# Expert tiles packed across two images: 39 tiles in place of 46, nine of them before the second image is routed

## The chip, the cores and the metric

The kernel runs on one core of a Trainium2 chip. The metric is the device time of one execution in microseconds (us), as the median of several executions. The core has five engines that run side by side and wait for each other through semaphores: TensorE (PE in the profile, PEld its weight loads), VectorE (DVE), ScalarE (ACT), GpSimd (POOL) and SyncE (SP). SP, ACT and POOL also issue DMAs.

## The reference, cut to what matters

Two images of 128 channels and 32 x 32 pixels pass through an attention block over pixels (4 heads), a linear attention block (8 heads) and a mixture of experts with top-2 routing. The last part is the one that the change touches:

```python
t = t + _L1_ffn_ref(_ln_t(t), Wr, br, ln_g, ln_b, W1, b1, W2, b2)    # t: 2 images x 1024 tokens x 128

def _L1_ffn_ref(x, Wr, br, ln_g, ln_b, W1, b1, W2, b2):             # E = 8 experts, hidden size 512
    probs = softmax(xt @ Wr + br)
    top_p, top_idx = top_k(probs, 2)
    weights = top_p / top_p.sum(axis=-1, keepdims=True)
    xn = (xt - mu) * rsqrt(var + LN_EPS)
    xe = xn[None] * ln_g[:, None, :] + ln_b[:, None, :]
    h = gelu(einsum('end,edh->enh', xe, W1) + b1[:, None, :])
    y = einsum('enh,ehd->end', h, W2) + b2[:, None, :]
    out = (weights[:, :, None] * y[chosen two experts]).sum(axis=1)
```

Every token goes to two of eight experts, so each image brings 2048 rows. How many rows an expert gets is known only at run time.

## The kernel before, in words

All is written by hand: each engine has one program, and the order in it is the order of the code. The image is called b (0 the first, 1 the second).

**Attention.** 64 steps (`UNITS * STEPS`) of scores on PE, exponentials on ACT (L558) and products with the values on PE (L864). Beside them a second stream finds the row maxima ahead of time (PE L806, L826; DVE L1189). These maxima go through `mrow` and two DMAs on SP (`max_rows`, L352) into `Qs`, and the scores of each half unit (L845) wait for them. From step 33 on (`LAYER1_AT`), the first image's later layers are spread between the steps: projection, linear attention, router, and at step 56 the counting.

**Routing, per image.** `v_slots(b)` on DVE turns the counts into a seat for each row in a table `expert_in` in DRAM (`xs`): rows of an expert stand together, each expert's share is padded to whole tiles of 128 rows, and each image has its own region of `TILES` = 23 tiles. POOL then writes the rows there with 16 indirect DMAs per image (`scatter`, L491: 8 token groups by 2 choices). The padding rows were written before, in `expert_in <- zeros` (L478); they hold zeros and the number of an unused result row. `v_slots` also makes `tab` (the expert of each tile), `etab` and `affine` (layer-norm scale and shift of each tile).

**The order on POOL.** Zero fill (L472 to L478), a wait for it, then `rsqrt` twice for the first image, `scatter(0)` with the first `rsqrt` of the second image (`rsqrt(B + 2)`) put before the last two of its 16 DMAs, `rsqrt(B + 3)`, four `send`s, `scatter(1)`, and the other 42 sends. Image 1's token layer norm (DVE L1239, `F`) waits for `rsqrt(B + 2)`.

**Expert tiles.** A loop over `NT` = 46 tiles runs on every engine (`expert_step`). For tile s: SP loads it into one of 8 buffers (`load_tile`, L378); PE transposes it (L1042); ACT copies it with the expert's scale and shift (L666); PE makes the hidden layer (L1068, four matmuls in two passes each); DVE adds the bias (`H`, L1469); ACT applies gelu (L684); PE makes the result of tile s - 1 (L1081); DVE adds its bias (`Y`, L1480); POOL sends it to DRAM rows (`send`, L496). The tiles of image 1 wait for all of `scatter(1)` (L389: `scattered[1]`), those of image 0 for `scatter(0)`. The second image's later layers (`LAYER1_PE`, `LAYER1_DVE`, `LAYER1_ACT`) are laid before and between the first six tile steps; its `v_slots` comes on DVE after tile step 4.

**The end.** SP waits for the sends, loads the results back (`load_sent`, L385), PE sums residual and gated results (L1098 to L1108), ACT copies, SP stores.

```python
TILES = (2 * L + E * (P - 1)) // P        # 23: the most tiles that one image can need
NT = B * TILES                            # 46
```

## Time and profile before

| | us |
|---|---|
| median of 3 runs (363.18 to 363.31) | 363.25 |
| span of the profiled execution | 384.2 |
| PE busy in it | 334.2 |
| DVE busy | 202.1 |
| ACT busy | 204.4 |
| POOL busy | 110.8 |

The profile is of one execution, and its span is 21 us longer than the median of the timed ones. The mean granted clock of TensorE over the span is 0.929 of the full 2.4 GHz; where it is below 1 it is at the lower of its two levels, 1.2 GHz, for part of the time. In the rows, a number in brackets behind a line is the time for which the engine sat idle before it, and an arrow names what ended that idle time; "remote" and "another core or an unknown queue" mean that the profile found no releaser, and "issue" that it shows nothing the engine waited for.

### The profile page before, as it was taken

Reading aid. Unit: us, or ns where it says so; the run is one execution under the profiler, and the core shown is the slowest. Engines: PE = TensorE matmul, PEld = TensorE weight load, DVE = VectorE, ACT = ScalarE, POOL = GpSimd, SP = SyncE. Lnnn points to the kernel's source line nnn. Section 1 sums busy time; section 2 is a strip of 40 time slices with the busy share of each in tenths; the row PEclk is TensorE's granted clock in tenths of the full one; section 3 lists DMA queues with packets and bytes.
Section 4 is the critical chain, followed back from the end, with each engine's and each line's share of the span. In section 5 each row is a group of like instructions: output and inputs, shape, how many; then the busy total and the mean of one; then the engine's idle time right before and its main releaser. Section 6 shows DMA issues by size and latency. Waiting matters only on the chain.

```text
span 384.2 us, 6582 instructions
## 1 busy us (share of the span) xinstructions
PE 334.2 (87%) x2004; PEld 211.5 (55%) x2004; DVE 202.1 (53%) x616; ACT 204.4 (53%) x324; POOL 110.8 (29%) x140
## 2 busy tenths in 40 slices
PE   7879799899999989999998496967551999999996
PEld 3533343333333335445432354867551999999996
DVE  2584444563756553565576248666402455777620
ACT  1460765666576554655585023665212677777732
POOL 2082291000000001000307630061774344444430
PEclk9985989999999999999999879996665899999999
DMA  6078768660000025000001102010211222222415
GB/s 186 2 149 194 170 146 333 154 243 34 0 2 3 3 72 149 0 2 1 2 0 43 55 8 62 16 28 23 62 62 34 64 72 70 71 66 79 143 37 210
DMA packets 21772, 29.28 MB, mean 76 GB/s; under 512 B 4055, under 2 KB 15628, under 8 KB 21484
## 3 DMA queue, kind: packets, MB, share of 16 engines
q1 hardware_dynamic: 16808, 18.04, 17.7%
q0 software_dynamic: 3744, 10.31, 8.4%
q10 hardware_dynamic: 1188, 0.53, 0.6%
q8 instruction: 17, 0.28, 0.3%
q14 instruction: 15, 0.12, 0.1%
HBM read 11.62 MB, written 9.25 MB: 54 GB/s over the span
## 4 chain that ended last, share of the span: by engine, by line
PE 70%; DVE 13%; issue 6%; another core or an unknown queue 4%; ACT 3%; DMA 1%; POOL 1%; DVEq 0%; SPq 0%; ACTq 0%; POOLq 0%
PE ps L864 15%; PE ps L1081 10%; PE ps L1068 9%; PE ps L845 6%; PE ps L826 6%; DVE above L1189 4%; PE ps L706 2%; PE ps L806 2%; PE ps L922 2%; PE ps L746 2%; PE ps L899 2%; PE ps L778 1%; PE ps L891 1%; DMA Qs<-mrow 1%
## 5 line engine op out<-in xcount | busy, mean ns | idle before, releaser
L558 ACT ACTIVATE probs<-ps 128x1024 f32<-128x1024 f32 x64 | 65.3, 1021 | 37.0 <-PE ps L845 36.9
L1081 PE MATMUL ps<-w,GT 128*128 x368 | 55.0, 297 | 18.8 <-ACT GT L684 15.0
L864 PE MATMUL ps<-probs,vT 128*32 128x512 f32 x256 | 68.2, 608 | 1.1 <-ACT probs L558 1.1
L864 PE MATMUL ps<-probs,ones 128*32 128x512 f32 x256 | 68.2, 609 | 0.0
L1081 PEld LDWEIGHTS ps<-w,GT 128*128 128x128 f32 x368 | 49.3, 208 | 22.0 <-issue 21.7
L1189 DVE CUSTOM_DVE_ANT_0 above<-ps,above 128x512 f32<-128x512 f32 x56 | 38.7, 691 | 40.8 <-PE ps L826 39.0
L496 POOL DMA_INDIRECT token_out<-Y,yidx x46 | 44.2, 961 | 48.2 <-DVE Y L1480 46.6
L433 POOL TENSOR_TENSOR rstd<-ve,minus_half 128x1 f32<-128x1 f32 (+2 forms) x6 | 10.3, 1724 | 160.6 <-DVE ve L1231 88.6
L1068 PE MATMUL ps<-XTT,w1s 128*128 128x128 f32 x368 | 53.1, 291 | 3.2 <-issue 3.2
L684 ACT ACTIVATE GT<-H 128x512 f32<-128x512 f32 x46 | 28.9, 629 | 46.5 <-DVE H L1469 27.4
L1068 PEld LDWEIGHTS ps<-XTT,w1s 128*128 128x128 f32 x368 | 49.2, 208 | 4.3 <-issue 4.3
L551 ACT ACTIVATE above<-ps 128x512 f32<-128x512 f32 x56 | 33.5, 599 | 25.3 <-PE ps L806 25.3
L1469 DVE TENSOR_TENSOR H<-ps,b1T 128x512 f32<-128x512 f32 x46 | 31.8, 691 | 27.8 <-PE ps L1068 7.4
L845 PE MATMUL ps<-Qs,Ks 98*128 98x512 f32 x128 | 44.0, 425 | 1.8 <-DMA Qs<-mrow 1.1
L845 PEld LDWEIGHTS ps<-Qs,Ks 98*128 98x128 f32 x128 | 21.8, 191 | 31.0 <-issue 23.7
L491 POOL DMA_INDIRECT expert_in<-X,slots x32 | 31.0, 969 | 25.4 <-DVE slots L1374 16.3
L826 PEld LDWEIGHTS ps<-Ks,Qs 96*128 96x128 f32 x56 | 10.6, 190 | 38.1 <-DVE pm L1189 32.8
L826 PE MATMUL ps<-Ks,Qs 96*128 96x512 f32 x56 | 28.0, 500 | 3.5 <-DVE pm L1189 1.4
L659 ACT ACTIVATE w1s<-w 128x512 f32 x46 | 28.5, 619 | 0.5 <-issue 0.4
L1480 DVE TENSOR_TENSOR Y<-ps,bias 128x128 f32<-128x128 f32 x46 | 13.3, 290 | 23.3 <-remote 11.1
L666 ACT ACTIVATE XTT<-ps,affine 128x128 f32<-128x128 f32 x46 | 20.3, 442 | 9.5 <-PE ps L1042 9.5
L806 PE MATMUL ps<-Kd,Qs 96*128 96x512 f32 x56 | 23.4, 418 | 1.0 <-ACT above L551 1.0
(196 smaller groups left out, 427.5 us busy)
## 6 DMA issues: line engine op xcount, KB each, us to landing
expert_in<-zeros POOLq DMA_DIRECT2D x2, 1495.0 KB, 7.6
XR<-expert_in SPq DMA_DIRECT2D x46, 65.0 KB
Qs<-q_hi SPq DMA_DIRECT2D x16, 128.0 KB, 3.1
w<-in_L_ffn_W SPq DMA_DIRECT2D x1, 2048.0 KB, 8.4
w<-in_L_ffn_W SPq DMA_DIRECT2D x8, 256.0 KB, 4.1
YG<-token_out SPq DMA_DIRECT2D x8, 256.0 KB, 4.1
Ks<-k_hi SPq DMA_DIRECT2D x14, 128.0 KB, 2.6
X<-in_x SPq DMA_DIRECT2D x2, 512.0 KB, 4.6
```

Source lines behind the costliest of these rows:

```text
L491: pool.indirect_dma_start(xs[:, :], bass.IndirectOffsetOnAxis(ap=slots[:, b, w, j:j + 1], axis=0), X2[:, b, j, :], None).then_inc(scattere ...
L496: pool.indirect_dma_start(yt[:, :], bass.IndirectOffsetOnAxis(ap=yidx[:, t:t + 1], axis=0), Y[:, t % NBY, :], None).then_inc(y_sent[t % NB ...
L551: nc.scalar.activation(above[:, n % 2, :], bank(slot_banks(g)[1]), ACT.Relu).then_inc(above_ready, 1)
L558: nc.scalar.activation(probs[:, s % 3, :], bank(2 + 2 * (s % 2), 2), ACT.Exp).then_inc(exp_done, 1)
L806: nc.tensor.matmul(bank(slot_banks(g)[1]), q, Kd[0:SPLIT, b, n, :], start=True, stop=True).then_inc(diff_ready, 1)
L826: last = nc.tensor.matmul(o, Qs[0:SPLIT, b, n, t * P:(t + 1) * P], Ks[0:SPLIT, b, n, HALF:L], start=True, stop=True)
L845: last = nc.tensor.matmul(bank(2 + 2 * (s % 2) + hd), Ks[0:STACK, b, n, kt * P:(kt + 1) * P], Qs[0:STACK, b, n, qh * HALF:(qh + 1) * HALF] ...
L864: last = nc.tensor.matmul(bank(6 + o % 2)[i * HD:(i + 1) * HD, :], w, probs[:, s % 3, hd * HALF:(hd + 1) * HALF], start=kt == 0, stop=kt = ...
L1068: last = nc.tensor.matmul(bank(2 + s % 2)[:, c * P:(c + 1) * P], w1s[:, s % 2, c, :], XTT[:, s % NB, :], start=True, stop=True)
L1081: last = nc.tensor.matmul(bank(4 + p)[:, 0:D], GT[:, p, c, :], w2[:, e, c, :], start=c == 0, stop=c == HC - 1)
L1189: nc.vector.tensor_tensor_reduce(above[:, n % 2, :], bank(base), above[:, n % 2, :], scale=1.0, scalar=-3.0e38, op0=ALU.add, op1=ALU.max, ...
L1469: nc.vector.tensor_tensor(H1[:, s % NB, :].rearrange("p (c t) -> p c t", c=HC), bank(2 + s % 2).rearrange("p (c t) -> p c t", c=HC), b1T[: ...
```

## The change

The two images no longer have a region each. `FULL` = 9 tiles is the least number of whole tiles that 2048 rows over 8 experts must contain; `REST` = 30 is the most that is then needed for all that is left of both images; `NT` = 39.

- `v_slots(0)` gives the first image's whole tiles the tiles 0 to 8 (whole tiles beyond the ninth, and each expert's incomplete rest, go to the tiles from 9 on, padded), in `seats_own`. It then notes where free seats are (`seats_left`).
- `v_slots(1)` puts the second image's rows into the free seats first and into new tiles behind them (`seats_filled`).
- Tiles 0 to 8 wait for `scatter(0)`, tiles 9 to 38 for `scatter(1)`.
- At the border the loop takes tiles in another order: after tile 8's hidden layer the results of tiles 7 and 8 are both made, and then the tiles 9 and 10 are fetched (`tiles_closed`, `tiles_fetched`).
- The zero fill has 39 tiles in place of 46, in two DMAs of 20 and 19 tiles from a smaller buffer, the second issued after the first has landed.
- The results of tiles 0 to 22 (`OWN`) are waited for before the first image's results are loaded back, as before.

The diff, cut to its core:

```diff
-    TILES = (2 * L + E * (P - 1)) // P
-    NT = B * TILES
+    OWN = (2 * L + E * (P - 1)) // P
+    FULL = -(-(2 * L - E * (P - 1)) // P)
+    REST = (B * 2 * L - FULL * P + E * (P - 1)) // P
+    NT = FULL + REST
+    TILE_RANGE = ((0, FULL), (FULL, NT))
+    ZT = 20
+    ZEROED = ((0, ZT), (ZT, NT))
...
+        def tiles_fetched(s):
+            if FULL - 2 <= s < FULL:
+                return (FULL, FULL + 1) if s == FULL - 1 else ()
+            return (s + 2,) if is_tile(s + 2) else ()
+
+        def tiles_closed(s):
+            if s == FULL - 1:
+                return (s - 1, s)
+            return () if s == FULL or not is_tile(s - 1) else (s - 1,)
...
             for t in range(NT):
-                if t % TILES == 0:
-                    sp.wait_ge(scattered[t // TILES], 16 * 2 * J)
+                if t in (0, FULL):
+                    sp.wait_ge(scattered[t // FULL], 16 * 2 * J)
                 load_tile(t)
...
-            for b in range(B):
-                v = xs[b * TILES * P:(b + 1) * TILES * P, :].rearrange("(p r) d -> p r d", p=P)
-                pool.dma_start(v, zeros[:, :, :]).then_inc(xs_zeroed, 16)
-            pool.wait_ge(xs_zeroed, 16 * B)
+            for i, (first, end) in enumerate(ZEROED):
+                rows = end - first
+                link(nc.gpsimd.iota(zeros[:, 0:rows, D], ...))
+                v = xs[first * P:end * P, :].rearrange("(p r) d -> p r d", p=P)
+                pool.dma_start(v, zeros[:, 0:rows, :]).then_inc(xs_zeroed, 16)
+                pool.wait_ge(xs_zeroed, 16 * (i + 1))
...
+            def seats_own(n):
+                link(nc.vector.tensor_copy(cnt_i[:, :], n))
+                whole_tiles(WHOLE)
+                running(CUM, WHOLE)
+                link(nc.vector.tensor_tensor(BEFORE, CUM, WHOLE, ALU.subtract))
+                nc.vector.tensor_scalar_min(CUTS, CUM, float(FULL * P))
+                link(nc.vector.tensor_scalar_min(AT, BEFORE, float(FULL * P)))
+                link(nc.vector.tensor_tensor(CUT, CUTS, AT, ALU.subtract))
+                link(nc.vector.tensor_tensor(LEFT, n, CUT, ALU.subtract))
+                link(nc.vector.tensor_scalar_add(cnt_i[:, :], LEFT, float(P - 1)))
+                whole_tiles(PAD)
+                running(CUMPAD, PAD)
+                link(... START ...)
+                link(nc.vector.tensor_tensor(SHIFT, START, CUT, ALU.subtract))
+                link(nc.vector.tensor_tensor(SHIFT, SHIFT, AT, ALU.subtract))
...
             def v_slots(b):
...
-                link(nc.vector.tensor_scalar_add(cnt_i[:, :], incl[:, :, J - 1], float(P - 1)))
-                link(nc.vector.tensor_scalar(cnt_i[:, :], cnt_i[:, :], 7, 7, ALU.arith_shift_right, ALU.logical_shift_left))
-                link(nc.vector.tensor_copy(cnt[:, 0, :], cnt_i[:, :]))
-                link(nc.vector.tensor_tensor_scan(cnt[:, 1, :], ones[:, 0:E], cnt[:, 0, :], 0.0, ALU.mult, ALU.add))
-                link(nc.vector.tensor_tensor(cnt[:, 2, :], cnt[:, 1, :], cnt[:, 0, :], ALU.subtract))
-                link(nc.vector.tensor_tensor(slotv, slotv, cnt[:, 2, :]..., ALU.add))
+                if b == 0:
+                    seats_own(incl[:, :, J - 1])
+                else:
+                    seats_filled(incl[:, :, J - 1])
                 link(nc.vector.tensor_tensor(slotv, slotv, ps[...], ALU.add))
+                link(nc.vector.tensor_tensor(past, slotv, over_j(CUT), ALU.is_ge))
+                nc.vector.tensor_tensor(slotv, slotv, over_j(AT), ALU.add)
+                link(nc.vector.tensor_tensor(past, past, over_j(SHIFT), ALU.mult))
+                link(nc.vector.tensor_tensor(slotv, slotv, past, ALU.add))
```

**DVE, first image's seats.** What stands between the running sum over the counts (L1361 before, L1433 after) and the first multiplication with the chosen experts (L1372, L1445). `xn` is scratch for the 64-wide seats, `cnt` for the 8-wide counts. Before:

```order
L1362 TENSOR_SCALAR cnt_i<-xn 128x8
L1363 TENSOR_SCALAR cnt_i<-cnt_i 128x8
L1364 CAST cnt<-cnt_i 128x8
L1365 SCALAR_TENSOR_TENSOR cnt<-ones,cnt 128x8
L1366 TENSOR_TENSOR cnt<-cnt 128x8
L1367 TENSOR_TENSOR xn<-xn,cnt 128x64
L1369 TENSOR_TENSOR xn<-xn,ps 128x64
```

Now, the last twelve of 21 rows (nine more 8-wide ones stand ahead of them):

```order
L1399 TENSOR_SCALAR cnt_i<-cnt 128x8
L1380 TENSOR_SCALAR cnt_i<-cnt_i 128x8
L1381 CAST cnt<-cnt_i 128x8
L1384 SCALAR_TENSOR_TENSOR cnt<-ones,cnt 128x8
L1402 SCALAR_TENSOR_TENSOR cnt<-cnt 128x8
L1403 TENSOR_TENSOR cnt<-cnt 128x8
L1404 TENSOR_TENSOR cnt<-cnt 128x8
L1438 TENSOR_TENSOR xn<-xn,ps 128x64
L1440 TENSOR_TENSOR xn<-xn,cnt 128x64
L1441 TENSOR_TENSOR xn<-xn,cnt 128x64
L1442 TENSOR_TENSOR xn<-xn,cnt 128x64
L1443 TENSOR_TENSOR xn<-xn 128x64
```

Seven operations have become 21 in all: sixteen 8-wide and five 64-wide ones. For the second image seven have become twelve (seven 8-wide, five 64-wide).

**PE, the border at tile 8.** `XR` is a loaded tile, `w1s` the staged first weights, `GT` the gelu's output. Before, from tile 8's hidden layer on:

```order
L1068 MATMUL ps<-XTT,w1s 128x128 x4
L1042 MATMUL ps<-ident,XR 128x128
L1051 TENSOR_LOAD tab
L1051 ISA x2
L1081 ISA
L1081 MATMUL ps<-w_52,GT 128x128
L1081 ISA
L1081 MATMUL ps<-w_52,GT 128x128
L1081 ISA
L1081 MATMUL ps<-w_52,GT 128x128
L1081 ISA
L1081 MATMUL ps<-w_52,GT 128x128
```

Now, from the end of tile 8's result (its last three matmuls) on:

```order
L1103 MATMUL ps<-w_52,GT 128x128
L1103 ISA
L1103 MATMUL ps<-w_52,GT 128x128
L1103 ISA
L1103 MATMUL ps<-w_52,GT 128x128
L1063 MATMUL ps<-ident,XR 128x128 x2
L1089 MATMUL ps<-XTT,w1s 128x128 x4
L1063 MATMUL ps<-ident,XR 128x128
L1089 MATMUL ps<-XTT,w1s 128x128 x4
L1063 MATMUL ps<-ident,XR 128x128
```

The transposes of tiles 9 and 10 have moved behind the results of tiles 7 and 8, and PE has no work in hand when it comes to them.

**POOL, the zero fill.** Before:

```order
L472 MEMSET zeros 128x2990
L473 IOTA zeros 128x23
L478 DMA expert_in<-zeros 128x2990 x2
L482 IOTA X_77 128x8 x2
L433 TENSOR_TENSOR rstd<-ve,minus_half 128x8
```

Now:

```order
L492 MEMSET zeros 128x2600
L496 IOTA zeros 128x20
L499 DMA expert_in<-zeros 128x2600
L496 IOTA zeros 128x19
L499 DMA expert_in<-zeros 128x2470
L503 IOTA X_77 128x8 x2
```

The two DMAs were issued back to back; now a wait and an IOTA stand between them.

## Rows read from the trace of the kernel before

**Rows 1.** The page: the chain that ended last, by engine.

```profile
PE 70%; DVE 13%; issue 6%; another core or an unknown queue 4%; ACT 3%; DMA 1%; POOL 1%; DVEq 0%; SPq 0%; ACTq 0%; POOLq 0%
```

**Rows 2.** The chain in order of time: start us, us, what (pieces of it).

```profile
146.82 1.79 PE ps L891 x16
...
296.47 2.07 PE ps L1081 x8
...
301.13 0.89 PE ps L1068 x8
...
366.24 0.91 PE ps L1068 x8
```

**Rows 3.** Timeline, attention's end to the first tile: start us, us, engine, line.

```profile
202.59 1.09 POOL L491 DMA_INDIRECT expert_in<-X,slots  x1 [12.04 <-DVE slots L1374]
...
211.78 2.05 PE L884 MATMUL ps<-ident,XP 128*128 128x128 f32 x16
...
216.12 0.72 DVE L1206 STREAM_TRANSPOSE rec<-ps 64x512 f32<-64x512 f32 x1 [8.09 <-remote]
...
218.96 3.78 PE L891 MATMUL ps<-wT,attn 128*128 128x128 f32 x16 [5.12 <-issue]
...
219.18 0.96 POOL L491 DMA_INDIRECT expert_in<-X,slots  x1 [0.30 <-issue]
...
222.53 6.43 PE L899 MATMUL ps<-XP,ident 128*128 128x512 f32 x12
...
225.83 1.67 POOL L433 TENSOR_TENSOR rstd<-ve,minus_half 128x8 f32<-128x8 f32 x1 [5.69 <-DVE ve L1231]
...
228.87 3.72 PE L922 MATMUL ps<-wT,F 128*128 128x256 f32 x16
...
229.09 0.97 POOL L491 DMA_INDIRECT expert_in<-X,slots  x1 [0.30 <-issue]
...
235.07 1.13 PE L1068 MATMUL ps<-XTT,w1s 128*128 128x128 f32 x8 [0.55 <-issue]
```

**Rows 4.** Timeline, tiles 5 to 9 and the second image's scatter.

```profile
268.69 0.95 POOL L491 DMA_INDIRECT expert_in<-X,slots  x1 [4.29 <-DVE slots L1374]
...
278.69 1.39 PE L1068 MATMUL ps<-XTT,w1s 128*128 128x128 f32 x8
...
282.20 0.69 DVE L1469 TENSOR_TENSOR H<-ps,b1T 128x512 f32<-128x512 f32 x1 [6.49 <-remote]
...
287.66 0.96 POOL L491 DMA_INDIRECT expert_in<-X,slots  x1 [0.30 <-issue]
...
294.14 0.29 DVE L1480 TENSOR_TENSOR Y<-ps,bias 128x128 f32<-128x128 f32 x1 [11.12 <-remote]
```

**Rows 5.** Busy by stretch: us, PE, PEld, DVE, ACT, POOL, clock, DMA share, GB/s.

```profile
218.50:225.30 6.80, 6.34 (x20) 4.78 (x21) 2.46 (x15) 2.35 (x4) 1.33 (x2) 0.54 0.06 20
...
283.30:300.30 17.00, 7.97 (x37) 7.43 (x38) 2.44 (x8) 4.00 (x9) 8.89 (x10) 0.51 0.15 47
```

**Rows 6.** Timeline of DVE in the first image's `v_slots`, and what follows it.

```profile
200.07 0.17 DVE L1365 TENSOR_TENSOR_SCAN cnt<-ones,cnt 128x8 f32<-128x8 f32 x1
...
200.48 0.22 DVE L1367 TENSOR_TENSOR xn<-xn,cnt 128x64 f32<-128x64 f32 x1
200.74 0.22 DVE L1369 TENSOR_TENSOR xn<-xn,ps 128x64 f32<-128x64 f32 x1
...
205.15 0.72 DVE L1206 STREAM_TRANSPOSE rec<-ps 64x512 f32<-64x512 f32 x1
```

**Rows 7.** The zero fill by its line, and the timeline beside it.

```profile
L478 POOL DMA_DIRECT2D expert_in<-zeros x2: 543/576/610, 58.1 to 58.7; - x2
...
DMA to landing us min/median/max: 6.0/7.6/9.2
...
62.73 1.92 SPq L352 DMA_DIRECT2D Qs<-mrow  x2
...
68.33 0.73 PE L845 MATMUL ps<-Qs,Ks 98*128 98x512 f32 x2 [1.12 <-DMA Qs<-mrow]
```

More of the change, by code:

```diff
@@ L1083, in expert_step @@
                     last.then_inc(y_ready, 1)
+                if s == FULL - 1:
+                    for t in tiles_fetched(s):
+                        x_transpose(t)
             pe.wait_ge(ld_w2, 16 * E)
@@ L1352, in v_choose, with whole_tiles, running, over_j @@
                 nc.vector.tensor_tensor(mask[:, :, :], hot[:, 0, :, :], hot[:, 1, :, :], ALU.add).then_inc(mask_ready, 1)
+            def whole_tiles(rows):
+                link(nc.vector.tensor_scalar(cnt_i[:, :], cnt_i[:, :], 7, 7, ALU.arith_shift_right, ALU.logical_shift_left))
+                link(nc.vector.tensor_copy(rows, cnt_i[:, :]))
+            def running(total, of):
+                link(nc.vector.tensor_tensor_scan(total, ones[:, 0:E], of, 0.0, ALU.mult, ALU.add))
+            def over_j(column):
+                return column.unsqueeze(2).broadcast_to([P, E, J])
@@ L1379, in v_slots @@
[L1379 to L1384 removed]
+                nc.vector.tensor_copy(slots[:, b, :, :], slotf[:, :, :]).then_inc(slots_ready, 1)
@@ new lines, in v_slots, with over_tiles @@
+                first, end = TILE_RANGE[b]
+                count = end - first
+                tiles, picked = cmp[:, 0:count, :], pick[:, 0:count, :]
+                def over_tiles(row):
+                    return row.unsqueeze(1).broadcast_to([P, count, E])
+                link(nc.vector.tensor_tensor(tiles, t_iota[:, 0:count, :], over_tiles(CUTS), ALU.is_ge))
+                link(nc.vector.tensor_reduce(tabf[:, 0:count], tiles, AX, ALU.add))
+                if b:
+                    link(nc.vector.tensor_tensor(tabf[:, :], tabf[:, :], own_tab[:, 0, :], ALU.add))
@@ L1385, in v_slots @@
+                link(nc.vector.tensor_scalar_min(etab[:, first:end], tabf[:, 0:count], float(E - 1)))
+                nc.vector.tensor_scalar_min(tab[0:1, first:end], tabf[0:1, 0:count], float(E - 1)).then_inc(tab_ready, 1)
+                link(nc.vector.tensor_tensor(tiles, over_tiles(iota_e[:, :]),
+                                             etab[:, first:end].unsqueeze(2).broadcast_to([P, count, E]), ALU.is_equal))
                 for i in range(2):
-                    link(nc.vector.tensor_tensor(pick, cmp, vcol[:, 5 + i * E:5 + (i + 1) * E].unsqueeze(1).broadcast_to([P, TILES, E]),
-                                                 ALU.mult))
@@ L1388, in v_slots @@
-                    last = nc.vector.tensor_reduce(affine[:, i, b * TILES:(b + 1) * TILES], pick, AX, ALU.add)
-                    if i == 0:
+                    link(nc.vector.tensor_tensor(picked, tiles, over_tiles(vcol[:, 5 + i * E:5 + (i + 1) * E]), ALU.mult))
+                    last = nc.vector.tensor_reduce(affine[:, i, first:end], picked, AX, ALU.add)
+                    if i == 0 or b == 0:
                         link(last)
-                last.then_inc(affine_ready, 1)
+                if b == 0:
+                    dve.sem_inc(affine_ready, 1)
+                    seats_left()
+                else:
+                    last.then_inc(affine_ready, 1)
```

102 lines of the change are left out of this document (55 added, 47 removed).

## The prediction

> **What bounds the kernel now.** I read the page's chain first [rows 1]: 70% of it is PE, and 4% is time that no releaser explains. Then the chain in order of time [rows 2]: once the tiles run freely, PE does one after the other, tile 11's hidden layer at 301.13 and tile 45's at 366.24. That is 65.1 us for 34 tiles, 1.91 us a tile, with no gap: there a tile less is worth its full price. The other limits are two places where PE stands: the end of the attention [rows 3] and the stretch in which the second image is routed and scattered [rows 4]. The change takes tiles away in the first kind of stretch and adds work or waiting to both of the others.
>
> **The trace against the timed runs.** The span is 384.2 us and the median 363.25, so at least 21 us of the rows aren't in a timed run. Three DVE waits without a releaser are the candidates. (a) L1206 sat idle for 8.09 us until 216.12; the attention's last products were done when PE went on to L884 at 211.78 [rows 3], so about 4.2 of it has no cause. (b) `H` of tile 7 came at 282.20 after 6.49 us, (c) `Y` of tile 6 at 294.14 after 11.12 us [rows 4]; what they wait for on PE stands ahead of tile 8's hidden layer, which starts at 278.69. I rebuild the program without them. After (a): o_used comes at 214.7, L891 follows, and at full clock its 16 matmuls take 1.79 (as at 146.82 [rows 2]) and not 3.78 [rows 3], the clock having fallen after PE's 5.12 us of idling [rows 5]. From L891's start to `rsqrt(B + 2)` it took 6.9 us (218.96 to 225.83), less the 2.0 just saved 4.9, so its variance would be there at 219.6. But POOL does 14 scatters first, the last from 219.18 to 220.14 [rows 3]. So `rsqrt` starts at 220.2 and not 225.83: 5.6 us less, and **POOL is what ends last there, by 0.6 us**. After (b) and (c): tile 7's `H` by 278.7, its result on PE behind tile 8's hidden layer (278.69 to 280.08), tile 9's hidden layer at 281.1, tile 11's at 284.9 in place of 301.13: 16.2 us less. 384.2 - 5.6 - 16.2 = 362.4, and 0.85 us is left for what lies around the span. That fits 363.25, and the sum below is made against this rebuilt program.
>
> **The change part by part.**
>
> *The seats of image 0 come later.* Between the running sum and the chosen experts DVE gets eleven more 8-wide operations and three more 64-wide ones. A waited-for 8-wide one costs 0.205 us (200.07 to 200.48 for two), a 64-wide one 0.26 (200.48 to 200.74) [rows 6]. One of each is not waited for; I put these at half. 10 x 0.205 + 0.1 + 2 x 0.26 + 0.14 = 2.8 us. The first scatter moves from 202.59 to 205.4, the fourteenth ends at 222.95, and `rsqrt(B + 2)` with all of image 1's layers, the last two scatters and tile 0 moves with it. The cover was lost already (POOL ends last): **+2.8 us**. If the timed runs keep the low clock in L891, the variance comes at 214.7 + 6.9 = 221.6 and the price is +1.4.
>
> *The rest of `v_slots(0)`* is nearly even: by estimates from the same prices, nine tiles in place of 23 in the table save 0.8 and the seven operations of `seats_left` cost 1.6. DVE's end of `v_slots(0)` moves by about 3.6, from 205.1 [rows 6] to 208.7, the normalisation before the last (2.8 us, as from 216.12 to L891's start at 218.96) to 211.5, and the last one can't start before 211.8 [rows 3]. Taken as nothing; if I miss three more operations here it is a few tenths.
>
> *PE idles longer before image 1's first layer.* L891 ends at 216.5 in the rebuilt program, the fillers (L899, 6.43 us, of which some 2.8 at the low clock, so 5.0 at full [rows 3, 5]) at 221.5. L922 starts 3.0 after `rsqrt` (225.83 to 228.87 [rows 3]): at 223.2 before, 226.0 now. The idling grows from 1.7 to 4.5 us. In the trace 5.12 us of it brought the clock to its lower level for 6.8 us [rows 5]. If it falls, L922's 3.7 us double in part, +1.7 (2.9 if the products behind it are slowed too); else nothing. I take the middle, **+0.9**.
>
> *The border at tile 9.* For image 1 `v_slots` gets two more 8-wide and three more 64-wide operations: 0.2 + 0.1 + 2 x 0.26 + 0.14 = 1.0 us. The first of `scatter(1)` moves from 268.69 to 269.7, the sixteenth from 287.66 to 288.6 [rows 4]. From the start of image 0's last scatter (229.09) to tile 0's hidden layer (235.07) it took 6.0 us [rows 3], 0.3 of it because PE was still busy: 5.7. Tile 9's hidden layer starts at 294.3. Before, it started at 281.1 in the rebuilt program, where tiles 9 to 15 filled just this time. **+13.2.** PE has done tile 8 by about 284 and stands for ten microseconds. On the restart after the trace's long wait the clock is at 0.51 until 300.3 [rows 5], and from 296.47 to 301.13 [rows 2] PE did what takes 2.8 at full clock: **+1.9**. Upper end: the low stretch after 218.50 lasted 6.8 us, which would cost 3.4.
>
> *What is saved.* Seven tiles by 1.91, 13.4 us, and tile 8's result, which is done in the wait, 0.95: **-14.3**. ACT and DVE lie beside PE, also with the 32 gate products, which now run beside the last sixteen tiles. The end (last send, load back, sum) keeps its shape: 0. Border together: 13.2 + 1.9 - 14.3 = +0.8.
>
> *The zero fill.* Before, 3.06 MB were queued at 58.1 and 58.7 and landed 6.0 and 9.2 us later, at 64.1 and 67.9; the row maxima, issued at 62.73, came only at 68.33, and PE waited 1.12 us [rows 7]. Now the first 1.33 MB land at about 63.6, the second part is issued about 64.3 and moves its data from 65.5 on; the two `mrow` DMAs (the second issued about 63.4) get through between. PE doesn't wait: **-1.1**. PE's chain behind it has no larger wait that would swallow this. If the second `mrow` DMA falls behind the second fill, it lands near 69.5: +1.1.
>
> **The sum.** 363.25 + 2.8 + 0.9 + 0.8 - 1.1 = 366.65, so **366.6 us**.
>
> A page bears on this. POOL's scatters run beside DVE in both places, with 1.28 us from one to the next in image 0 (202.59 to 219.18, 13 steps, DVE busy for the first third) and 1.265 in image 1 (268.69 to 287.66, 15 steps, DVE mostly idle) [rows 3, 4]: DVE's work doesn't slow them. The Trainium skill, "SBUF — State Buffer", section "Who interferes with whom", says that DVE in a two-port mode and GpSimd contend for one pair of ports and "the other **fully blocks**"; by this rule the added DVE operations, and in a timed run the `H` and `Y` of tiles 5 to 8, would hold up the scatters. The trace doesn't bear it out, so it is no part of the sum, and it is the third rival.
>
> **The rivals.**
>
> 1. *The scatters are quicker in a timed run than in the profiled one*, as the 21 us suggest that profiling costs something where POOL issues densely. At 0.96 us, without the 0.30 between two [rows 3], `scatter(1)` ends 4.5 us sooner and `rsqrt(B + 2)` waits for its variance as before, so that the 2.8 and the 0.9 go: 363.25 - 1.1 + 0.8 - 4.5 = 358.5. Each 0.1 us is worth 1.5 at tile 9 and about 1.3 at `rsqrt`; from a step of about 1.15 us down the change is faster. Against it: every duration that I can compare (1.91 a tile, the rebuilt 362.4) fits the timed median without it. Chance 0.17.
>
> 2. *Much of it is covered*: the low clock makes the variance of image 1 late anyway (+1.4), PE's clock doesn't fall, the row maxima come early by their whole wait of PE's weight load too (-1.6). 363.25 + 1.4 + 0.8 - 1.6 = 363.9. With the tile border a little cheaper this is no change. Chance 0.10.
>
> 3. *DVE's work slows the scatters*: with 0.3 us on each of sixteen and half of that on the first fourteen, 366.6 + 4.8 + 2.1 = 373.5; half as much gives 370. Against it the even steps above. Chance 0.05.
>
> **How the numbers follow.** The forecast, 366.6, has 0.68; its own terms reach from 364 to 369.5 (0 to 2.9 for the clock at L922, 1.9 to 3.4 at the restart, -1.1 to +1.1 at the zero fill). The range from 361.5 to 370.0 takes in the second rival and the nearer part of the first and leaves out some 0.17. About 0.2% (0.7 us) is what a measurement of this kernel can tell from no change. Faster 0.17, same 0.10, slower 0.73.
>
> **What would show it.** In the changed kernel's profile: 39 of each tile group and 1.91 us a tile from about tile 11; SP's load of tile 9 only behind the sixteenth scatter, some 19 us behind `slots` of image 1; PE idle for 10 us in front of the transposes of tiles 9 and 10, then a granted clock near 0.5 for 4 to 7 us; `rsqrt(B + 2)` directly behind the fourteenth scatter; no wait of L845 for `mrow` near 68 us. The waits (b) and (c) of DVE, if they come again, fall into the time in which PE waits for tile 9, so that the span may shrink by ten microseconds and more where the timed median grows; the span is no measure here. I am wrong if tile 9's load comes sooner than 17 us behind `slots`, or if tile 9 doesn't find PE idle.

## The result and the profile after

| | us |
|---|---|
| kernel before, median of 4 runs (363.18 to 363.99) | 363.28 |
| changed kernel, median of 4 runs (368.82 to 370.01) | 369.52 |
| ratio, 95% interval | 1.0172, 1.0151 to 1.0193 |
| profiled execution of the changed kernel: its own time / its span | 370.01 / 368.2 |

The change made the kernel 6.2 us slower. The prediction said 3.35 us slower (366.6, range 361.5 to 370.0), so sign and range held and the size was short by 2.9 us. The profiled execution is the longest of the four, with 1.8 us around its span: its rows can be compared with the median, give or take 0.5 us. Below, one execution of the kernel with border fillers (600.02 us) and one of the kernel with key fillers (506.95) lie far from all others; they count in the medians given, not in the ratios, and without them these medians are 365.74 and 368.85.

The chain that ended last, by engine, in the changed kernel's page:

```profile
PE 66%; DVE 14%; POOL 8%; issue 7%; ACT 2%; DMA 1%; DVEq 0%; POOLq 0%; ACTq 0%
```

Against [rows 1] POOL has grown from 1% to 8%, and the 4% without a releaser are gone. The pieces of that chain around the two places (start, us, what):

```profile
204.79 1.09 POOL expert_in L512
222.35 1.69 POOL rstd L453
...
287.22 2.33 DMA expert_in<-X,slots
289.56 1.84 DMA XR<-expert_in
```

The first image's scatters are in the chain up to `rsqrt(B + 2)` (L453), and the second image's up to the load of tile 9. (L943 makes the second image's values, L951 its transposed keys, L1089 the hidden layers: tile 2's starts at 248.00.) The timeline of the first place, which answers [rows 3]; start, us, engine, line, and in brackets the idle time before it:

```profile
204.79 1.09 POOL L512 DMA_INDIRECT expert_in<-X,slots  x1 [14.81 <-DVE slots L1447]
...
221.36 0.96 POOL L512 DMA_INDIRECT expert_in<-X,slots  x1 [0.30 <-issue]
222.35 1.68 POOL L453 TENSOR_TENSOR rstd<-ve,minus_half 128x8 f32<-128x8 f32 x1
...
225.39 5.41 PE L943 MATMUL ps<-wT,F 128*128 128x256 f32 x16 [4.17 <-DVE F L1264]
...
237.31 1.97 PE L951 MATMUL ps<-ident,xn 128*128 128x128 f32 x8 [2.79 <-ACT xn L591]
...
248.00 1.05 PE L1089 MATMUL ps<-XTT,w1s 128*128 128x128 f32 x8
```

And of the border, which answers [rows 4]; image 1's first and last scatter, the transposes of tiles 9 and 10, and the hidden layers of tiles 9 and 38:

```profile
268.16 0.96 POOL L512 DMA_INDIRECT expert_in<-X,slots  x1 [3.70 <-DVE slots L1447]
...
287.22 0.95 POOL L512 DMA_INDIRECT expert_in<-X,slots  x1 [0.30 <-issue]
...
291.45 0.95 PE L1063 MATMUL ps<-ident,XR 128*128 128x128 f32 x2 [9.67 <-DMA XR<-expert_in]
292.54 2.07 PE L1089 MATMUL ps<-XTT,w1s 128*128 128x128 f32 x8
...
349.68 1.06 PE L1089 MATMUL ps<-XTT,w1s 128*128 128x128 f32 x8
```

Busy time by stretch (us, PE, PEld, DVE, ACT, POOL, granted clock, DMA share, GB/s), which answers [rows 5]:

```profile
238.00:244.00 6.00, 6.00 (x35) 6.00 (x33) 3.43 (x6) 3.80 (x5) 0.00 (x0) 0.58 0.07 15
284.00:291.00 7.00, 0.00 (x0) 0.00 (x0) 0.00 (x0) 0.00 (x0) 5.17 (x6) 0.50 0.19 57
291.00:298.00 7.00, 6.41 (x29) 5.83 (x30) 1.64 (x4) 3.60 (x8) 2.87 (x3) 0.52 0.43 114
298.00:340.00 42.00, 41.98 (x375) 41.56 (x373) 27.40 (x83) 32.42 (x66) 20.91 (x22) 1.00 0.28 76
```

Between 284 and 291 us PE does nothing while POOL scatters and tile 9 is loaded, it works at the lower clock for as long again, and only then runs the tiles without a gap. The zero fill went as its step said ([rows 7]; POOL's timeline): POOL waits 4.54 us for the first fill, and then comes the number column and the second fill.

```profile
62.11 0.17 POOL L496 IOTA zeros<- 128x19 f32 x1 [4.54 <-DMA expert_in<-zeros]
62.58 0.58 POOL L499 DMA_DIRECT2D expert_in<-zeros  x1 [0.30 <-POOL zeros L496]
```

### The profile page after: what moved, and what is told of

Same layout as the page of the kernel before. It is cut to its first block, busy times and chain, and to the rows that moved or that the text cites. A ratio compares the mean times of both kernels' runs of the same rounds, so it can differ in the third digit from the quotient of the medians.

```text
span 368.2 us, 6156 instructions
## 1 busy us (share of the span) xinstructions
PE 319.2 (87%) x1885; PEld 195.7 (53%) x1885; DVE 199.2 (54%) x622; ACT 194.5 (53%) x303; POOL 104.1 (28%) x134
## 4 chain that ended last, share of the span: by engine, by line
PE 66%; DVE 14%; POOL 8%; issue 7%; ACT 2%; DMA 1%; DVEq 0%; POOLq 0%; ACTq 0%
PE ps L885 15%; PE ps L1089 9%; PE ps L1103 8%; POOL expert_in L512 8%; PE ps L847 7%; PE ps L866 5%; DVE above L1214 4%; PE ps L943 2%; PE ps L727 2%; PE ps L827 2%; PE ps L799 2%; PE ps L767 1%; DVE pm L1217 1%; PE ps L958 1%; PE ps L1063 1%
## 5 line engine op out<-in xcount | busy, mean ns | idle before, releaser
L453 POOL TENSOR_TENSOR rstd<-ve,minus_half 128x1 f32<-128x1 f32 (+2 forms) x6 | 10.3, 1723 | 158.2 <-DVE ve L1256 82.5
L1103 PE MATMUL ps<-w,GT 128*128 x312 | 44.4, 288 | 8.7 <-ACT GT L705 8.4
L1089 PE MATMUL ps<-XTT,w1s 128*128 128x128 f32 x312 | 46.1, 296 | 5.0 <-issue 4.9
L517 POOL DMA_INDIRECT token_out<-Y,yidx x39 | 37.5, 961 | 39.9 <-DVE Y L1561 37.8
L1089 PEld LDWEIGHTS ps<-XTT,w1s 128*128 128x128 f32 x312 | 42.2, 210 | 6.4 <-issue 6.0
L1103 PEld LDWEIGHTS ps<-w,GT 128*128 128x128 f32 x312 | 40.1, 201 | 10.3 <-issue 10.0
L866 PE MATMUL ps<-Qs,Ks 98*128 98x512 f32 x128 | 44.0, 425 | 0.7 <-issue 0.7
L1551 DVE TENSOR_TENSOR H<-ps,b1T 128x512 f32<-128x512 f32 x39 | 27.0, 692 | 31.9 <-PE ps L1089 28.7
L705 ACT ACTIVATE GT<-H 128x512 f32<-128x512 f32 x39 | 24.6, 629 | 29.1 <-DVE H L1551 29.0
L512 POOL DMA_INDIRECT expert_in<-X,slots x32 | 31.1, 971 | 27.5 <-DVE slots L1447 18.5
L866 PEld LDWEIGHTS ps<-Qs,Ks 98*128 98x128 f32 x128 | 21.9, 191 | 29.9 <-issue 23.7
L687 ACT ACTIVATE XTT<-ps,affine 128x128 f32<-128x128 f32 x39 | 17.1, 442 | 25.9 <-PE ps L1063 25.9
L680 ACT ACTIVATE w1s<-w 128x512 f32 x39 | 24.2, 620 | 1.1 <-issue 1.1
L885 PEld LDWEIGHTS ps<-probs,vT 128*32 128x32 f32 x256 | 9.8, 109 | 21.2 <-issue 17.9
```

What stands on the lines that cost most here:

```text
L512: pool.indirect_dma_start(xs[:, :], bass.IndirectOffsetOnAxis(ap=slots[:, b, w, j:j + 1], axis=0), X2[:, b, j, :], None).then_inc(scattere ...
L517: pool.indirect_dma_start(yt[:, :], bass.IndirectOffsetOnAxis(ap=yidx[:, t:t + 1], axis=0), Y[:, t % NBY, :], None).then_inc(y_sent[t % NB ...
L866: last = nc.tensor.matmul(bank(2 + 2 * (s % 2) + hd), Ks[0:STACK, b, n, kt * P:(kt + 1) * P], Qs[0:STACK, b, n, qh * HALF:(qh + 1) * HALF] ...
L885: last = nc.tensor.matmul(bank(6 + o % 2)[i * HD:(i + 1) * HD, :], w, probs[:, s % 3, hd * HALF:(hd + 1) * HALF], start=kt == 0, stop=kt = ...
L1089: last = nc.tensor.matmul(bank(2 + s % 2)[:, c * P:(c + 1) * P], w1s[:, s % 2, c, :], XTT[:, s % NB, :], start=True, stop=True)
L1103: last = nc.tensor.matmul(bank(4 + p)[:, 0:D], GT[:, p, c, :], w2[:, e, c, :], start=c == 0, stop=c == HC - 1)
```

## The experiments

Each timed kernel ran beside the kernel before (median 363.2 to 363.5 in the three series), and what counts is its distance from that; the changed kernel's is +6.2.

### The kernel before, profiled again

> The kernel before, unchanged, for a second trace. My rebuilt program (the three DVE waits without a releaser taken out) says: span about 361.5 to 362.5, rsqrt(B + 2) directly behind the fourteenth scatter at about 220.2, L891's matmuls at full clock, tile 9's hidden layer 12.4 us behind the first scatter of image 1. The rival, that the waits belong to the program, says: they come again at the same places and the span is 384 again.

363.61 us, span 361.8. The three waits of DVE without a releaser didn't come, and this is the program that the prediction had to rebuild. PE and POOL in its timeline:

```profile
201.75 1.09 POOL L491 DMA_INDIRECT expert_in<-X,slots  x1 [12.04 <-DVE slots L1374]
...
219.34 1.68 POOL L433 TENSOR_TENSOR rstd<-ve,minus_half 128x8 f32<-128x8 f32 x1
...
222.32 5.38 PE L922 MATMUL ps<-wT,F 128*128 128x256 f32 x16 [2.20 <-DVE F L1239]
...
234.21 1.09 PE L930 MATMUL ps<-ident,xn 128*128 128x128 f32 x8 [2.79 <-ACT xn L570]
...
242.53 1.05 PE L1068 MATMUL ps<-XTT,w1s 128*128 128x128 f32 x8
...
262.87 0.96 POOL L491 DMA_INDIRECT expert_in<-X,slots  x1 [4.28 <-DVE slots L1374]
...
275.07 1.06 PE L1068 MATMUL ps<-XTT,w1s 128*128 128x128 f32 x8
...
343.72 1.06 PE L1068 MATMUL ps<-XTT,w1s 128*128 128x128 f32 x8
```

The operation that writes the input of `rsqrt(B + 2)` ended at 217.39, so POOL came last there by 1.9 us, not by 0.6 (in the changed kernel it ended at 218.50, and POOL came last by 3.8). With this profile the 6.4 us between the spans (361.8 and 368.2) can be laid out stage by stage:

| stage | before | after | more | predicted |
|---|---|---|---|---|
| start to the first scatter (201.75; 204.79) | 201.75 | 204.79 | +3.0 | +2.8 - 1.1 |
| first scatter to `rsqrt(B + 2)` | 17.59 | 17.56 | 0 | 0 |
| `rsqrt(B + 2)` to image 1's first scatter | 43.53 | 45.81 | +2.3 | +0.9 + 1.0 |
| image 1's first scatter to tile 9's hidden layer | 12.20 | 24.38 | +12.2 | +12.2 |
| tile 9's to the last hidden layer | 68.65 | 57.14 | -11.5 | -14.3 + 1.9 |
| last hidden layer to the end | 18.1 | 18.5 | +0.4 | 0 |
| sum | | | +6.4 | +3.4 |

### The second zero fill behind the first, in the kernel before

```diff
                 pool.dma_start(v, zeros[:, :, :]).then_inc(xs_zeroed, 16)
-            pool.wait_ge(xs_zeroed, 16 * B)
+                pool.wait_ge(xs_zeroed, 16 * (b + 1))
```

> The kernel before with one edit: the second zero-fill DMA is issued only after the first has landed. My term says -1.0 us (PE's wait for the row maxima near 68 us goes), so 362.3. The rival, that later waits swallow it or the second fill blocks the row maxima instead, says 0 to +1.

362.25 us, ratio 0.9969 (0.9953 to 0.9985), 1.3 us less. The size is the expected one, but the profiles don't show it at the place: PE's matmuls waited for `mrow` neither here nor in the kernel before profiled again (there only a weight load of L845 did, for 0.24 us), and from DVE's first instruction to the first scatter it took 194.4 in this one (6.70 to 201.09) and 194.3 in that one (7.44 to 201.75). The 1.12 us of [rows 7] stood in one of the three profiles that have the two fills back to back. The spans of these two profiles differ by 1.3 us as well, but at other places: 0.7 lies ahead of DVE's first instruction (6.70 and 7.44), and 0.5 between `rsqrt(B + 2)` and image 1's first scatter, where the low clock fell elsewhere. In this profile the values (L922) and the transposed keys (L930) ran so:

```profile
221.60 3.72 PE L922 MATMUL ps<-wT,F 128*128 128x256 f32 x16 [2.15 <-DVE F L1239]
...
231.84 1.97 PE L930 MATMUL ps<-ident,xn 128*128 128x128 f32 x8 [2.79 <-ACT xn L570]
```

What the 1.3 us of the timed runs are made of stays open.

### The added seat operations alone, in the kernel before

```diff
                 link(nc.vector.tensor_tensor(cnt[:, 2, :], cnt[:, 1, :], cnt[:, 0, :], ALU.subtract))
+                if b == 0:
+                    nc.vector.tensor_scalar_min(more[:, 1, :], cnt[:, 1, :], 1152.0)
+                    for i in range(10):
+                        link(nc.vector.tensor_tensor(more[:, 0, :], cnt[:, 1, :], cnt[:, 2, :], ALU.subtract))
+                    nc.vector.tensor_tensor(wide[:, 2, :, :], incl, tot, ALU.add)
+                    for i in range(2):
+                        link(nc.vector.tensor_tensor(wide[:, i, :, :], incl, tot, ALU.add))
```

> The kernel before with eleven 8-wide and three 64-wide DVE operations more in the first image's v_slots, ahead of its slots, on scratch memory of their own. My theory (POOL's scatters end last in front of rsqrt(B + 2)) says +2.8 us, and +1.7 more if PE's longer idling drops its clock before L922: 366.1 to 367.8. The rival, that POOL has slack there, says at most +1.4: 364.7 or less.

367.90 us, ratio 1.0117 (1.0092 to 1.0142): 4.4 us for 2.8 us of DVE work (POOL's idle time ahead of the first scatter is 14.80 and not 12.04). Nothing of the packing is in this kernel, and yet 4.4 of the 6.2 us are. Its timeline (L924 are the values, L932 the transposed keys, L1070 tile 2's hidden layer):

```profile
222.52 1.68 POOL L435 TENSOR_TENSOR rstd<-ve,minus_half 128x8 f32<-128x8 f32 x1
...
225.56 5.72 PE L924 MATMUL ps<-wT,F 128*128 128x256 f32 x16 [5.00 <-DVE F L1241]
...
237.79 1.97 PE L932 MATMUL ps<-ident,xn 128*128 128x128 f32 x8 [2.80 <-ACT xn L572]
...
248.44 1.05 PE L1070 MATMUL ps<-XTT,w1s 128*128 128x128 f32 x8
```

`rsqrt` comes 3.2 us later than in the kernel before: 2.8 are the added operations, and 0.4 stand ahead of them. The values ran in part at the low clock in both (5.72 and 5.38 us, 3.72 at full), so my term for them is 0.3 at most. But from the keys to tile 2's hidden layer it takes 10.65 us here and 8.32 there (234.21 to 242.53): **a drop of the clock at the keys, 2.3 us**. The changed kernel has it too (237.31 to 248.00, 10.69). Not all of it is new time: from `rsqrt(B + 3)` to image 1's first scatter the kernel before took 16.67 us, with PE at a granted clock of 0.50 from 254 to 258, and this kernel 15.30, so 1.4 came back. Nor is it shown that the added operations cause the drop: the kernel with the fill in turn has none of them, and its keys took 1.97 us too, with 10.85 from there to tile 2.

### PE kept busy at the border, in the changed kernel

```diff
                 if s == FULL - 1:
+                    for i in range(10):
+                        nc.tensor.matmul(bank(0), ident[:, :], XP[:, 1, 0:4, :]..., start=True, stop=True)
                     for t in tiles_fetched(s):
                         x_transpose(t)
```

> The changed kernel with ten 128x512 filler matmuls on PE ahead of the transposes of tile 9, where PE otherwise idles 10 us. If the low clock after the idling costs 1.9 us or a little more, as I put it, the time falls from 369.5 to about 367.6. If the clock isn't the price there, it stays at 369.5; if the fillers run past the landing of tile 9, it grows.

365.97 us, ratio 1.0077 (1.0048 to 1.0107): +2.4 where the changed kernel had +6.2. PE in its timeline (L1108 are the fillers):

```profile
236.42 1.09 PE L951 MATMUL ps<-ident,xn 128*128 128x128 f32 x8 [2.79 <-ACT xn L591]
...
244.73 1.05 PE L1089 MATMUL ps<-XTT,w1s 128*128 128x128 f32 x8
...
279.81 8.75 PE L1108 MATMUL ps<-XP,ident 128*128 128x512 f32 x20
289.37 0.33 PE L1063 MATMUL ps<-ident,XR 128*128 128x128 f32 x1 [0.82 <-DMA XR<-expert_in]
...
290.31 1.16 PE L1089 MATMUL ps<-XTT,w1s 128*128 128x128 f32 x8
...
345.66 1.06 PE L1089 MATMUL ps<-XTT,w1s 128*128 128x128 f32 x8
```

From tile 9 to tile 38 it now takes 55.35 us and not 57.14: the low clock behind the border costs 1.8, as expected (1.9). The other 2 us that this profile is shorter lie ahead of the edit: 0.7 ahead of the first scatter (0.6 of it ahead of DVE's first instruction), and 1.4 between `rsqrt(B + 2)` and image 1's first scatter (44.41 for 45.81). There the clock stayed full at the keys (8.31 us from 236.42 to 244.73), with the same code up to there, and the next low stretch was at tile 5 (2.05 us for its hidden layer) and not at tile 4 (2.05 in the changed kernel's profile). So whether it drops at the keys differs between executions of equal code. The rows also give the second part of the restart. At 1.907 us a tile (64.85 us for the 34 tiles from tile 11's hidden layer at 278.87 to tile 45's at 343.72 in the kernel before profiled again), 28 tiles and 0.95 for the one that has no result ahead of it make 54.35. With the fillers 1.0 is left over, with the granted clock at 1.00 from 290.3 on, so it isn't the clock but the empty pipeline: PE has nothing between the hidden layers of tiles 9 and 10, and result 9 waits for its gelu. In the changed kernel the restart costs 2.8 in all.

### Three fillers ahead of the keys; ten ahead of the values in place of six

```diff
             def t_keyT(b):
+                if b:
+                    for i in range(3):
+                        nc.tensor.matmul(bank(6), ident[:, :], XP[:, 1, 0:4, :]..., start=True, stop=True)
                 pe.wait_ge(ek_ready, b + 1)
```

In this kernel the fillers write over the transposed rows of tile 2 in bank 6, so tile 2's results are not the right ones.

> The changed kernel with three 128x512 matmuls of no use put on PE ahead of the second image's transposed keys (L951), where PE idles for 2.8 us (234.5 to 237.3). Theory (clock at the keys): from the keys to tile 2's hidden layer the changed kernel's profile took 10.69 us (237.31 to 248.00) with the clock at its lower level, and the kernel before took 8.32 (234.21 to 242.53) with it full; this is a part of the miss. PE kept busy up to the keys holds the clock: about 2.4 us less, 367.1. Rival A (what the clock does there is chance and not idleness, the timed executions are a mix): less than 1 us gained, 368.5 to 369.5. Rival B (the fillers themselves run at half pace and hold up the keys by up to 2.6 us): 370 to 372.

369.01 us, ratio 1.0139 (1.0112 to 1.0166), +5.6: 0.6 less than the changed kernel, which is what rival A said.

```diff
-    FILLERS = 6
+    FILLERS = 10
```

> The changed kernel with ten of the 128x512 fillers (L920) ahead of the second image's values (L943) in place of six: 3.5 us more PE work in a wait of 4.17 us. In the profiles both kernels run L943 at the lower clock (5.38 us before, 5.41 after, 3.7 at full). Theory (idleness drops the clock): L943 in 3.7 us, 1.7 us less, 367.8, if the clock does not fall at the keys instead, where PE still idles 2.8 us. Rival A (the clock falls anyway at one of the two places, so that only its place moves): 369.5, no change, perhaps 0.7 slower. My prediction had 0.9 for a longer wait here; by the two profiles it was worth nothing.

367.26 us, ratio 1.0105 (1.0079 to 1.0131), +3.8: 2.4 less. Its profiled execution was the longest of its five, with 369.24. The values and the keys, first with three fillers at the keys, then with ten at the values:

```profile
226.03 6.75 PE L943 MATMUL ps<-wT,F 128*128 128x256 f32 x16 [4.09 <-DVE F L1268]
...
239.30 1.09 PE L955 MATMUL ps<-ident,xn 128*128 128x128 f32 x8 [0.22 <-ACT xn L591]
```

```profile
226.03 3.72 PE L943 MATMUL ps<-wT,F 128*128 128x256 f32 x16 [0.73 <-DVE F L1264]
...
236.26 1.97 PE L951 MATMUL ps<-ident,xn 128*128 128x128 f32 x8 [2.79 <-ACT xn L591]
```

Behind each filled wait the products ran at full clock. With the values' wait filled, the keys pay. With the keys' wait filled, the values are slow as well (6.75 us, 5.41 in the changed kernel), but they come ahead of these fillers in PE's program, so the edit can't be the cause: it is one more difference between executions of equal code. Nor do the full keys prove the fillers: in the profiles with the border fillers and with the sooner gates (below) they ran in 1.09 us with no filler ahead of them.

### Both waits filled

The two edits together, the three fillers at the keys in bank 3, which is free there.

> The changed kernel with both idle times of PE around the second image's first products filled: ten fillers (L920) in place of six, and three more of the same kind ahead of the transposed keys (L951). Either alone only moved the low clock: with ten fillers L943 ran in 3.72 us and the keys then took 1.97 for 1.09, with three fillers at the keys L943 took 6.75 and the keys 1.09. Theory (idleness drops the clock, and the missing 2.4 us at the keys are a second drop): with both filled neither drops, 1.7 + 2.4 less than the changed kernel, 365.4. Rival (the fillers only choose the place, one drop comes anyway): 367.2, as with the ten alone.

366.87 us, ratio 1.0086 (1.0062 to 1.0109), +3.6: 2.6 less than the changed kernel and 1.5 short of the theory. PE in its timeline (L1093 are hidden layers):

```profile
225.75 3.72 PE L943 MATMUL ps<-wT,F 128*128 128x256 f32 x16 [0.66 <-DVE F L1268]
...
235.99 1.09 PE L955 MATMUL ps<-ident,xn 128*128 128x128 f32 x8 [0.22 <-ACT xn L591]
...
244.31 1.05 PE L1093 MATMUL ps<-XTT,w1s 128*128 128x128 f32 x8
...
257.77 2.05 PE L1093 MATMUL ps<-XTT,w1s 128*128 128x128 f32 x8 [0.54 <-issue]
```

At both places the clock is full, and the keys to tile 2 take 8.32 us again. The timed runs side with the rival: it said 367.2, as with the ten fillers alone, and against those the three at the keys gave 0.2 us. In the profile, from the first scatter of image 0 to that of image 1 only 3.0 of the expected 4.1 us are gained (63.37 to 60.39): a later hidden layer, tile 5's at 257.77, has its matmuls at the low clock instead, as in the two profiles where the keys were at full clock without fillers. So of the filling only the part at the values is shown (2.4 us in timed runs with the ten alone); how much of the rest only moves stays open.

### rsqrt ahead of the last four scatters

```diff
-            scatter(0, lambda j: rsqrt(B + 2) if j == J - 1 else None)
+            scatter(0, lambda j: rsqrt(B + 2) if j == J - 2 else None)
```

> The changed kernel with rsqrt(B + 2) on POOL after the twelfth scatter instead of the fourteenth. Its input is ready at 218.5, the fourteenth scatter ends at 222.3, the twelfth at 219.8. Theory (POOL is what ends last there, so that the later seats of the first image cost their full 2.8 us): rsqrt and all behind it come 2.5 us sooner; tile 0 waits for all sixteen scatters and comes 2.3 us after them in the profile, so of this chain 2.5 are gained up to the second image's seats: 367.0. Rival (tile 0 or the scatters of the first image are what sets the time of the second image's layers): less than 1 us gained, 368.5 to 369.5.

364.36 us, ratio 1.0042 (1.0024 to 1.0060), +0.9: **5.3 less than the changed kernel**, twice what was expected. Its timeline:

```profile
203.54 1.09 POOL L512 DMA_INDIRECT expert_in<-X,slots  x1 [14.82 <-DVE slots L1447]
...
218.58 1.69 POOL L453 TENSOR_TENSOR rstd<-ve,minus_half 128x8 f32<-128x8 f32 x1
...
221.56 3.72 PE L943 MATMUL ps<-wT,F 128*128 128x256 f32 x16 [1.58 <-DVE F L1264]
```

From the first scatter to `rsqrt` it takes 15.04 us for 17.56: 2.5 less, the two scatters that it no longer waits for. PE idles 1.58 us and not 4.17 ahead of the values, and they run at full clock: another 1.7. (Idle time alone doesn't tell the clock: the values took 3.72 us behind 2.15 us of it with the fill in turn, and 5.38 behind 2.20 in the kernel before.) From `rsqrt` to image 1's first scatter it takes 44.00 us for 45.81, 1.8 less, and that has the 1.7 in it. Together 4.3 of the 5.3 us; where the last 1.0 lies isn't shown. Rows and timed runs agree that POOL sets the time of everything behind it here.

### The gates four tile steps sooner

```diff
-                if 0 <= s - (NT - 2 * J) < 2 * J:
-                    i = s - (NT - 2 * J)
+                if 0 <= s - (NT - 2 * J - 4) < 2 * J:
+                    i = s - (NT - 2 * J - 4)
```

> The changed kernel with the sixteen gate products of DVE (L1566) four tile steps sooner, so that none stands ahead of the last H. In the changed kernel's profile it is 18.5 us from the last tile's hidden layer to the end, 18.1 before: the last result on PE starts 3.15 us after its hidden layer and not 2.70. Theory: the gates cost 0.45 us in the tail, so 369.1. Rival (another cause, a transfer at the end): 369.5. The difference is near what the runs can tell; the profile decides.

369.38 us, ratio 1.0174 (1.0151 to 1.0197), +6.0. Its keys in the profile:

```profile
236.22 1.09 PE L951 MATMUL ps<-ident,xn 128*128 128x128 f32 x8 [2.79 <-ACT xn L591]
```

In the profile it is 18.4 us from the last hidden layer (347.90) to the end of the span (366.3): 0.1 of the 0.4 came back. The gates are not the cause of the longer tail; what is wasn't found.

### Both kernels mended

Last, whether packing pays once both kernels have the edits that gained. The changed kernel with the border fillers and the sooner `rsqrt`:

> The changed kernel with the two edits that gained most: rsqrt(B + 2) after the twelfth scatter (369.5 to 364.4) and ten fillers ahead of the transposes of tiles 9 and 10 (its profile showed 1.8 us less from tile 9 to the last tile). Theory (two separate places, so the gains add up, 5.2 + 1.8): 362.5. Rival (the 3.5 us that the timed runs gave to the border fillers are all at the border): 360.9. Rival (the two share one gain, since an earlier start changes where the clock falls): 364 and above.

363.40 us, ratio 1.0015 (0.9996 to 1.0034). On top of the sooner `rsqrt` the border fillers gain 0.8 us in the timed runs; the 3.8 that they gave to the changed kernel were mostly not at the border. The kernel before with the fill in turn and the sooner `rsqrt`:

> The kernel before with the second zero fill issued after the first has landed and rsqrt(B + 2) after the twelfth scatter. In its profile the input of rsqrt is there at 217.4 and rsqrt starts at 219.34, 1.9 us late. Theory (POOL ends last there in the kernel before too, so that the cover of 0.6 us that I reckoned with was none): 363.5 - 1.3 for the fill - 1.9 = 360.3, and a shorter idle time of PE ahead of L922 may give 1 more. Rival (the variance ends last): 362.2, as with the fill alone. Against the changed kernel with the same edits it tells what the packing itself is worth: by the first profiles it loses 12.2 and saves 11.5 at the tiles and pays 2.8 + 1.0 for the seats.

359.95 us, ratio 0.9911 (0.9894 to 0.9928), the fastest of all. And the changed kernel with the sooner `rsqrt`, border fillers, eight fillers ahead of the values, one ahead of the keys and the sooner gates:

> The changed kernel with everything that gained: rsqrt(B + 2) after the twelfth scatter, eight fillers in place of six ahead of L943, one ahead of the keys (L951), ten at the border, the gate products four tile steps sooner. Theory (the gains add up: 5.2, 1.8, up to 2.4 if the clock holds at the keys, 0.2): 360.0. Rival (one clock drop comes anyway): 362.3. Rival (fillers hold up real work): 364 and more. Below 360.3, what the mended kernel before should give, packing would be worth having.

361.85 us, ratio 0.9982 (0.9963 to 1.0001). The timelines of the mended kernel before and of the changed kernel with the two edits, each with `rsqrt`, image 1's first scatter and tile 9's hidden layer:

```profile
216.89 1.67 POOL L433 TENSOR_TENSOR rstd<-ve,minus_half 128x8 f32<-128x8 f32 x1 [0.70 <-DVE ve L1231]
...
257.97 0.96 POOL L491 DMA_INDIRECT expert_in<-X,slots  x1 [2.92 <-DVE slots L1374]
...
270.21 1.06 PE L1068 MATMUL ps<-XTT,w1s 128*128 128x128 f32 x8
```

```profile
219.21 1.68 POOL L453 TENSOR_TENSOR rstd<-ve,minus_half 128x8 f32<-128x8 f32 x1
...
263.24 0.96 POOL L512 DMA_INDIRECT expert_in<-X,slots  x1 [3.70 <-DVE slots L1450]
...
287.39 1.16 PE L1089 MATMUL ps<-XTT,w1s 128*128 128x128 f32 x8
```

In the first, `rsqrt` waits for its variance (0.70), so POOL no longer ends last there. Tile 9 is 12.24 us behind image 1's first scatter in the first and 24.15 in the second, 11.9 more; from tile 9 to the end of the span it takes 86.9 (to 357.1) and 74.0 (to 361.4), 12.9 less. So the border itself now gains 1.0 us, and the seats of both images and what hangs on them cost 5.3 (263.24 - 257.97); 1.8 of that is the clock from the keys to tile 2 (10.49 and 8.70 us). With equal edits, and the border fillers besides, packing loses 3.5 us in the timed runs (363.40 to 359.95), and 1.9 with all fillers on its side alone.

## Why the prediction was right, and where it was short

1. **The trace against the timed runs.** Right. Taking out the three waits of DVE gave 362.4 for the span, and the profile without them has 361.8. Around a span lie 1.7 to 1.9 us in every run, not 0.85: what I took for a fit was the remainder, and the rebuilt program was some 0.9 us too long.
2. **POOL ends last at `rsqrt(B + 2)`.** Right and decisive, by 1.9 us and not 0.6. The seats of image 0 cost their full DVE time, 2.77 us (idle time ahead of the first scatter 12.04 and 14.81), and moving `rsqrt` alone gave back most of the slowdown (and 2.0 us in the kernel before).
3. **PE idles longer ahead of the values, +0.9.** About the right size by luck, at the wrong place. The idle time grew as worked out (2.20 to 4.17; I had 1.7 to 4.5), but the values were in part at the low clock before and after (5.38 and 5.41 us), which costs nothing new. The profiles differ behind them: the changed kernel lost 2.4 at the keys and got 1.4 back behind `rsqrt(B + 3)`, where a low stretch held up the kernel before (254 to 258), so the clock cost 1.0 net. With the 1.2 for the seats of image 1 (`rsqrt(B + 3)` to its first scatter takes 16.48 in the changed kernel, 15.30 with the operations of image 0 alone) the stage grew by 2.3 where 1.9 was forecast. In two other executions of the same code up to there it grew by only 0.9 (44.41), so what the longer idle time itself costs stays open. The seat operations alone cost 4.4 us in timed runs for 2.8 of work.
4. **The border.** The delay was right to a tenth, 12.2 us without the seats, and PE stood for 9.67 us. The 24.38 us from image 1's first scatter to tile 9's hidden layer are 19.1 us of scatters, 2.33 until the last has landed, 1.84 for the load and 1.1 for transposes and copy. The saving of 14.3 was right as well. The term that was mis-sized is the restart, 1.9 forecast and 2.8 measured: the clock's part was right (1.8), but 1.0 for the empty pipeline was not in the sum.
5. **The zero fill, -1.1.** The wait was not there in the second profile of the kernel before, so nothing of it shows between the two profiles: the start grew by 3.0, not by 1.7. This is the largest single miss of the rows (1.3 of 3.0): a wait of one execution was priced as if each had it. In timed runs of the kernel before, though, the edit gave 1.3 at places not found, so the size came out and the reason given for it did not.
6. **The tail, 0.** It was +0.4; the gates explain 0.1 of it.
7. **The range.** The measured 369.5 lies just inside it, and "its own terms reach from 364 to 369.5" doesn't follow from the terms: with each at its end they reach from 365.75 (only the 0.9 can go down) to 372.35 (2.0, 1.5 and 2.2 more).
8. **The rivals.** Quicker scatters in timed runs: no, the step is 1.27 us in the changed kernel (268.16 to 287.22, 15 steps), as in [rows 4]. Much covered: no, POOL ended last by more than I had reckoned. DVE's work slows the scatters: by 0.1 us at most, and not as the rival had it. The added seat operations stand ahead of the scatters, and `seats_left` and the layer norms run beside them, with the same 1.275 us a step (204.79 to 221.36, 13 steps) as in [rows 3]. In image 1 two steps were longer in all nine profiles of the changed kernel and its variants, 1.34 and 1.32 us beside the table operations of DVE, which have become wider (128x240 for 128x184), where the kernel before has 1.28 and 1.27. The Trainium skill, "SBUF — State Buffer", section "Who interferes with whom", lets GpSimd and a DVE instruction in a two-port mode hold each other up for the whole instruction, and it gives `tensor_tensor`, which `H`, `Y` and most of the added operations are, no such mode: with two SBUF inputs it contends with GpSimd's reads, no more. The prediction read it too widely. No run here shows a scatter held up for as long as a DVE instruction beside it.

What was said to show it came: 39 tiles, 1.91 us each from tile 11 on, `rsqrt` directly behind the fourteenth scatter, no matmul of L866 waiting near 68, the load of tile 9 21.7 us behind image 1's `slots` (289.56 - 267.88; I had some 19), and 14 us at 0.50 to 0.52 of the clock, 7 of them with PE at work.

As an estimate from the single edits and the rows, 5.4 of the 6.2 us are accounted for: 4.4 for the seats of image 0 with the clock behind them (timed), 1.2 for the seats of image 1, 1.1 for border and tail (12.2 - 11.5 + 0.4), less 1.3 for the fill (timed). The border by itself, without the seats, was not run.

## What to carry to other kernels

Work that is added ahead of a chain can cost more than its own time when an engine idles behind it (here 4.4 us for 2.8): look at each longer wait for both the step that follows it and the ones after, because the clock may drop at the next wait and not at this one. Take more than one profile of the same code before a price is put on a drop, since its place differs from one execution to the next. Before a change is built on a place where an engine ends last, the order on that engine should be tried: here one instruction put ahead of two more scatters was worth 5.3 us in the changed kernel and 2.0 in the old one (-1.3 and -3.3 against its start), while seven tiles fewer were worth 1.0 at best. Taking work away at the end of a program by making its middle wait for a whole transfer pays only by what the pipeline had left to do in that time, and a restart costs the refilling as well as the clock.
